# Last batch of an attention and feed-forward layer: tiles 4 and 5 turned by VectorE and moved inside SBUF in place of TensorE transposes, with other orders around them

## The chip, the cores and the metric

The kernel runs on one core of one Trainium2 chip. The metric is the device time of one execution, in microseconds (us); the figure quoted is the median of three runs. Five queues of instructions run side by side: TensorE (PE in the profile, its weight loads PEld), VectorE (DVE), ScalarE (ACT), GpSimd (POOL) and SyncE (SP), which issues nearly all DMAs. Each works through its own queue in order, and they wait for one another through semaphores.

## The reference

For 8 batches of 1024 rows of width 512, all in float32:

```
x  = x + layernorm(attn(layernorm(x)))
x  = x + layernorm(ffn(layernorm(x)))

attn(x): s  = sigmoid(silu(x @ s_w1.T + s_b1) @ s_w2.T + s_b2)
         u  = (x @ B_w.T + B_b) * s
         h  = h @ A.T + u_t            (a scan over the rows; 128 states)
         y  = hs @ C_w.T + C_b + x @ D_w.T + D_b
         return y * sigmoid(x @ g_w.T + g_b)
ffn(x):  square(relu(x @ Ws1)) @ Ws2   + a routed part weighted by trunc(prob)
```

The routed part counts only for rows whose largest probability reaches 1. A bound on the router's weights (`router_gap`, `route_flag`) tells at the end of the run whether any row can; if none can, that part is skipped, as in the runs shown.

## The kernel before

**Tiles.** A batch is 8 tiles (0 to 7) of 128 rows by 512. Batches run one after another; the last one has order lists of its own, `last_tail` and `last_body`, one in each engine's block, written out by hand call by call. What an engine does next is therefore fixed by these lists, and a call waits for its inputs with everything that stands behind it on that engine.

**One tile's way through the last batch.** TensorE computes the gate `G(j)` and the attention output `Y(j)`. ScalarE takes the sigmoid (`gate`). VectorE multiplies (`attn`, L1315), takes mean and variance (`v_bn`, `v_ag`, `v_ep`), subtracts the mean (`less_v_mean`), and adds the scaled result to x (`x1_sum`, L1346). GpSimd raises the variance to the power -1/2 in between (`v_rs`, L1942). Then VectorE takes the statistics of the sum (`x1_bn`, `x1_ag`, `x1_ep`), GpSimd makes scale and shift (`x1_rs`), and ScalarE writes the normed tile to `work` (`x1_norm`, L935).

**Turning a tile.** The feed-forward matmuls need the tile transposed, in a high part `x2T_hi` and a low part `x2T_lo` (float32 as two reduced parts, so each product is three matmuls, `mm3`, L499 to L501). Tiles 0 to 3 of the last batch, and all tiles of earlier batches, go this way: VectorE transposes 32x32 blocks into `x2q` (`turn`, L1369); when both tiles of a pair are there, SyncE issues four DMAs that carry the blocks to their partitions, back into `work` (`move`, L425); ScalarE copies the high part (`t_hi`, L926); GpSimd subtracts for the low part (`t_low`, L1997). Tiles 4 to 7 of the last batch go another way: `x1_norm` writes them with their columns permuted, TensorE transposes into PSUM banks (`T`, L579), ScalarE copies the high part from there (`t_hi`, L923), and VectorE subtracts (`t_low`, L1362).

**The feed-forward part.** `W1f(m, f)` (12 matmuls) multiplies half f of the hidden width for the four tiles of group m; its f = 0 call waits for the low part of the group's last tile. ScalarE applies relu and square (`hidden`, L968 and L971), VectorE squares in full precision and subtracts for the low part (`h2`, L1418 and L1422). `W2(j)` (6 matmuls) gives the output of tile j; `W2(0)` waits for `h2(0, 1)`. The output is normed (`z_bn`, `z_ag`, `z_ep` on VectorE, `z_rs` on GpSimd, `zn` on ScalarE), added to x (`outs` on GpSimd, `last_outs` and `very_last_out` on VectorE), and stored by SyncE.

**The order around the change.** On TensorE the last batch ends Y(4) to Y(7), W1f(0,0), W1f(0,1), T(4), T(5), W2(0), T(6), W2(1), T(7), W2(2), W1f(1,0), W1f(1,1), the router's matmuls, W2(3) to W2(7). On GpSimd it has `v_rs(5)`, `t_low(2)`, `t_low(3)`, `v_rs(6)`. On VectorE `h2(0,0)` stands behind `v_ep(7)` and ahead of `x1_sum(7)`, and `h2(0,1)` behind `x1_bn(7)`. `move` is called for tiles 0 to 3 only.

Of the kernel before, what the change touches and what calls it, by code (L numbers as in the profile page):

```python
# [18 lines left out]
def build(nc, x, xt, A, AT, BwT, Bb, CwT, Cb, DwT, Db, s1T, s1b, s2T, s2b, gwT, gb, Ws1p, Ws1, Ws2, W1, W2, Wr, eye, out):  # L19
    NB, T, D = x.shape  # L20
# [18 lines left out]
    with ExitStack() as ctx:  # L39
# [241 lines left out]

        def tr_bank(name):
            return TR[int(name[1]) % len(TR)]
# [77 lines left out]
        def _(eng):  # L361
# [65 lines left out]
            def one_pass(b, rep):  # L427
                if rep == 0:

                    eng.wait_ge(*lo_of("g"))  # L430
                    eng.wait_ge(*lo_of("d"))
                for m in range(NM):
                    js = slice(m * MS, (m + 1) * MS)
                    if rep > 0:
                        if m == NM - 1:
                            store_out(b - 1, 2)
                            store_out(b - 1, 3)
                        eng.wait_ge(S["x1_st" + str(m)], body_at("x1_st" + str(m), b - 1))
                        eng.wait_ge(S["out_ok"], body_at("out_ok", b - 1, m * MS + MS - 1))
                    eng.dma_start(xres[:, js, :], x_v[b][:, js, :]).then_inc(S[f"xres_ld{m}"], 16)  # L440
                    if rep + 1 < NB:
                        norm_rows(b, m)
                for m in range(NM):
                    js = slice(m * MS, (m + 1) * MS)
                    if rep + 1 < NB or m == 0:
                        move(b, 2 * m)
                    if rep + 2 < NB:
                        load_next_x(b + 2, m)
                    if rep + 1 < NB or m == 0:
                        move(b, 2 * m + 1)  # L450
                    eng.wait_ge(S["x1_ok"], body_at("x1_ok", b, m * MS + MS - 1))
                    eng.dma_start(x1_v[b][:, js, :], xres[:, js, :]).then_inc(S[f"x1_st{m}"], 16)
                store_out(b, 0)
                store_out(b, 1)
# [40 lines left out]
        def _(eng):  # L495
# [86 lines left out]
            def T(b, rep, j):  # L582

                if j >= MS + len(TR):
                    eng.wait_ge(S["t_lo"], body_at("t_lo", b, j - len(TR)))
                eng.wait_ge(S["xn2_ok"], body_at("xn2_ok", b, j))
                transposes(tr_bank(f"t{j}"), work[:, j, :]).then_inc(S["t_done"], 1)
# [181 lines left out]
            def last_body(b, rep):  # L769
                a = (b, rep)  # L770
                Y(*a, 0)
                G(*a, 4)
                Y(*a, 1)
                G(*a, 5)
                Y(*a, 2)
                Y(*a, 3)
                G(*a, 6)
                G(*a, 7)
                Y(*a, 4)
                Y(*a, 5)  # L780
                Y(*a, 6)
                Y(*a, 7)
                W1f(*a, 0, 0)
                W1f(*a, 0, 1)
                T(*a, 4)
                T(*a, 5)
                W2(*a, 0)
                T(*a, 6)
                W2(*a, 1)
                T(*a, 7)  # L790
# [88 lines left out]
        def _(eng):  # L879
# [32 lines left out]
            def t_hi(b, rep, j):  # L912
                if rep == NB - 1 and j >= MS:
                    eng.wait_ge(S["t_done"], j - MS + 1)
                else:
                    wait_moved(eng, b, j)
# [5 lines left out]
                if rep == NB - 1 and j >= MS:  # L922
# [5 lines left out]
            def x1_norm(b, rep, j):  # L928
                eng.wait_ge(S["x1_nm"], body_at("x1_nm", b, j))
                dst, src = work[:, j, :], xres[:, j, :]  # L930
                if rep == NB - 1 and j >= MS:

                    dst = dst.rearrange("p (k r q) -> p k q r", k=KD, q=4)
                    src = src.rearrange("p (k q r) -> p k q r", k=KD, q=4)
# [156 lines left out]
            def last_body(b, rep):  # L1091
                a = (b, rep)
                gate(*a, 4)
                hs(*a, 2)
                gate(*a, 5)
                hs(*a, 3)
                hs(*a, 4)
                x1_norm(*a, 0)
# [5 lines left out]
                x1_norm(*a, 3)  # L1104
                hs(*a, 6)
                t_hi(*a, 1)
                gate(*a, 7)
                hs(*a, 7)
                t_hi(*a, 2)
                t_hi(*a, 3)  # L1110
                x1_norm(*a, 4)
                hidden(*a, 0, 0)
                x1_norm(*a, 5)
                hidden(*a, 0, 1)
                t_hi(*a, 4)
                x1_norm(*a, 6)
                t_hi(*a, 5)
                x1_norm(*a, 7)
# [87 lines left out]
        def _(eng):  # L1206
# [507 lines left out]
            def last_body(b, rep):  # L1714
                a = (b, rep)
                attn(*a, 0)
                attn(*a, 1)
                v_bn(*a, 0)
                hs_low(*a, 2)
                v_bn(*a, 1)  # L1720
                v_ag(*a, 0)
                v_ep(*a, 0)
                less_v_mean(*a, 0)
                v_ag(*a, 1)
                v_ep(*a, 1)
                x1_sum(*a, 0)
                less_v_mean(*a, 1)
                hs_low(*a, 3)
                x1_sum(*a, 1)
                x1_bn(*a, 0)  # L1730
                x1_bn(*a, 1)
                x1_ag(*a, 0)
                x1_ep(*a, 0)
                attn(*a, 2)
                x1_ag(*a, 1)
                x1_ep(*a, 1)
                v_bn(*a, 2)
                hs_low(*a, 4)
                v_ag(*a, 2)
                v_ep(*a, 2)  # L1740
                attn(*a, 3)
                less_v_mean(*a, 2)
                x1_sum(*a, 2)
                turn(*a, 0)
                turn(*a, 1)
                v_bn(*a, 3)
                hs_low(*a, 5)
                v_ag(*a, 3)
                v_ep(*a, 3)
                less_v_mean(*a, 3)  # L1750
                x1_bn(*a, 2)
                x1_ag(*a, 2)
                x1_ep(*a, 2)
                x1_sum(*a, 3)
                x1_bn(*a, 3)
                x1_ag(*a, 3)
                x1_ep(*a, 3)
                turn(*a, 2)
                attn(*a, 4)
                turn(*a, 3)  # L1760
                hs_low(*a, 6)
                v_bn(*a, 4)
# [4 lines left out]
                x1_sum(*a, 4)  # L1767
                v_bn(*a, 5)
                v_ag(*a, 5)
                hs_low(*a, 7)  # L1770
# [5 lines left out]
                v_bn(*a, 6)  # L1776
                x1_ag(*a, 4)
                v_ag(*a, 6)
                x1_bn(*a, 5)
                x1_ep(*a, 4)  # L1780
                v_ep(*a, 6)
                less_v_mean(*a, 6)
                x1_ag(*a, 5)
                attn(*a, 7)
                v_bn(*a, 7)
                x1_sum(*a, 6)
                x1_ep(*a, 5)
                v_ag(*a, 7)
                x1_bn(*a, 6)
                less_v_mean(*a, 7)  # L1790
                x1_ag(*a, 6)
                v_ep(*a, 7)
                h2(*a, 0, 0)
                x1_sum(*a, 7)
                x1_ep(*a, 6)
                x1_bn(*a, 7)
                h2(*a, 0, 1)
                x1_ag(*a, 7)
                x1_ep(*a, 7)
                t_low(*a, 4)  # L1800
                t_low(*a, 5)
                z_bn(*a, 0)
                z_ag(*a, 0)
                z_ep(*a, 0)
                t_low(*a, 6)
                z_bn(*a, 1)
                t_low(*a, 7)
# [64 lines left out]
            h2(NB, NB, 1, 0)  # L1872
            z_ag(NB - 1, NB - 1, 2)
            z_ep(NB - 1, NB - 1, 2)
            h2(NB, NB, 1, 1)
            z_bn(NB - 1, NB - 1, 3)
            z_ag(NB - 1, NB - 1, 3)
# [7 lines left out]
            route_flag()  # L1885
# [49 lines left out]
        def _(eng):  # L1935
# [142 lines left out]
            def last_body(b):  # L2078
                v_rs(b, 0)
                v_rs(b, 1)  # L2080
                x1_rs(b, 0)
                v_rs(b, 2)
# [8 lines left out]
                t_low(b, 2)  # L2091
                t_low(b, 3)
                v_rs(b, 6)
# [4 lines left out]
                x1_rs(b, 7)  # L2098
                z_rs(b, 0)
# [69 lines left out]
```

## Time and profile before

| what | value |
|---|---|
| median of 3 runs | 800.47 us (800.14 to 800.48) |
| the profiled execution, its own time | 800.6 us |
| its span, first to last instruction | 798.6 us |
| TensorE busy | 783.3 us (98% of the span) |
| VectorE, GpSimd, ScalarE busy | 605.9, 456.4, 344.4 us |
| mean granted TensorE clock | 0.998 |

The profile is one execution, so times on its axis are compared with its own 800.6 us; it lies 0.13 us above the median. The last batch begins near 699 us, and the lists that the change touches work from about 729 us to the end. In a timeline each row is one instruction, or several alike that were merged (x2, x8); rows of VectorE and ScalarE that follow without a wait overlap a little, so that the step from one start to the next is shorter than the duration.

### The profile page before, as it was taken

To read this page: it belongs to the slowest core of one execution; us is meant where nothing else is said; L and a number is where in the kernel's file an instruction comes from. 1 tells how busy PE (TensorE), PEld (TensorE's weight loads), DVE (VectorE), ACT (ScalarE), POOL (GpSimd) and SP (SyncE) were. 2 spreads that over 40 slices of the span, in tenths; PEclk is the share of its full clock that TensorE was granted. 3 is DMA by queue.
4 is the path that set the end of the run, shared out by engine and by line. 5 is a ranking of instruction groups with operands and counts; after the bars stand their busy time and mean duration, and the time that the engine had idled before them with its cause. 6 is when DMAs were issued, how large, how long until landed. Compare 5 with 4: busy or idle time off the path is not lost. (4 is left out here: it accounts for less than half of the span.)

```text
span 798.6 us, 10778 instructions
## 1 busy us (share of the span) xinstructions
PE 783.3 (98%) x3628; PEld 648.0 (81%) x3628; DVE 605.9 (76%) x1404; ACT 344.4 (43%) x554; POOL 456.4 (57%) x553
## 2 busy tenths in 40 slices
PE   7999999999999999999999999999999999999996
PEld 6878888888888888888888888888888888888875
DVE  7868896598956897678975889649896589734895
ACT  4535354344434554245443535435443444432353
POOL 1253658548465576466674665845757557644445
PEclk9999999999999999999999999999999999999999
DMA  8534434454355425552345533454425442232222
GB/s 269 207 107 158 137 94 138 160 184 134 87 177 174 161 89 158 183 187 80 95 143 185 185 101 96 147 185 168 149 80 182 150 143 80 78 133 87 65 113 106
DMA packets 40767, 110.90 MB, mean 139 GB/s; under 512 B 7044, under 2 KB 24836, under 8 KB 32903
## 3 DMA queue, kind: packets, MB, share of 16 engines
q1 hardware_dynamic: 40278, 110.00, 41.4%
q8 instruction: 29, 0.48, 0.3%
q10 hardware_dynamic: 432, 0.20, 0.1%
q14 instruction: 28, 0.22, 0.1%
HBM read 60.84 MB, written 33.61 MB: 118 GB/s over the span
## 5 line engine op out<-in xcount | busy, mean ns | idle before, releaser
L499 PE MATMUL TM<-gw_hi,xT_hi 128*128 128x512 f32 x256 | 107.3, 419 | 0.0
L1982 POOL TENSOR_TENSOR xres<-work,xres 128x512 f32<-128x512 f32 x56 | 75.1, 1341 | 52.8 <-DVE work L1332 52.8
L501 PE MATMUL TM<-gw_hi,xT_lo 128*128 128x512 f32 x256 | 100.6, 393 | 0.0
L501 PE MATMUL TM<-dw_hi,xT_lo 128*128 128x512 f32 x256 | 100.2, 391 | 0.0
L500 PE MATMUL TM<-gw_lo,xT_hi 128*128 128x512 f32 x256 | 100.0, 391 | 0.0
L499 PE MATMUL TM<-dw_hi,xT_hi 128*128 128x512 f32 x256 | 99.9, 390 | 0.0
L500 PE MATMUL TM<-dw_lo,xT_hi 128*128 128x512 f32 x256 | 99.6, 389 | 0.0
L996 ACT ACTIVATE work<-TM,nmz,rsz 128x512 f32<-128x512 f32 x62 | 48.2, 777 | 106.7 <-POOL nmz L1952 106.7
L1942 POOL TENSOR_TENSOR rsv<-rsv,negh 128x1 f32<-128x1 f32 x64 | 47.1, 736 | 82.3 <-DVE rsv L1328 82.2
L1997 POOL TENSOR_TENSOR x2T_lo<-work,x2T_hi 128x512 fp32r<-128x512 f32 x60 | 78.5, 1319 | 2.0 <-ACT x2T_hi L926 1.9
L1990 POOL TENSOR_TENSOR work<-work,xres 128x512 f32<-128x512 f32 x60 | 76.7, 1295 | 1.3 <-ACT work L996 1.3
L1315 DVE TENSOR_TENSOR work<-TM,work 128x512 f32<-128x512 f32 x64 | 44.0, 687 | 43.9 <-PE TM L501 43.9
L1942 POOL TENSOR_TENSOR rsz<-rsz,negh 128x1 f32<-128x1 f32 x64 | 35.5, 555 | 59.1 <-DVE rsz L1470 58.5
L935 ACT ACTIVATE work<-xres,nmx,rsx 128x512 f32<-128x512 f32 x64 | 54.0, 843 | 32.8 <-POOL nmx L1952 32.7
L1254 DVE TENSOR_TENSOR xin<-xin,norm_row 128x1024 f32<-128x1024 f32 x56 | 66.1, 1211 | 0.4 <-ACT norm_row L941 0.3
L1942 POOL TENSOR_TENSOR rsx<-rsx,negh 128x1 f32<-128x1 f32 x64 | 40.6, 635 | 39.7 <-DVE rsx L1359 39.7
L926 ACT ACTIVATE x2T_hi<-work 128x512 fp32r<-128x512 f32 x60 | 36.1, 625 | 57.1 <-DMA work<-x2q 57.1
L501 PEld LDWEIGHTS TM<-gw_hi,xT_lo 128*128 128x128 f32 x256 | 48.0, 188 | 10.9
L501 PEld LDWEIGHTS TM<-dw_hi,xT_lo 128*128 128x128 f32 x256 | 48.1, 188 | 10.1
L500 PEld LDWEIGHTS TM<-dw_lo,xT_hi 128*128 128x128 f32 x256 | 48.1, 188 | 10.0
L499 PEld LDWEIGHTS TM<-dw_hi,xT_hi 128*128 128x128 f32 x256 | 48.1, 188 | 10.0
L901 ACT ACTIVATE work<-TM 128x512 f32<-128x512 f32 x64 | 37.2, 591 | 41.6 <-PE TM L501 36.3
(189 smaller groups left out, 2063.1 us busy)
## 6 DMA issues: line engine op xcount, KB each, us to landing
xres<-in_x SPq DMA_DIRECT2D x16, 1024.0 KB, 5.9
x_scratch<-xres SPq DMA_DIRECT2D x16, 1024.0 KB, 4.7
xin<-in_x SPq DMA_DIRECT2D x15, 1024.0 KB, 5.3
work<-x2q SPq DMA_DIRECT2D x120, 128.0 KB, 2.7
out<-work SPq DMA_DIRECT2D x30, 512.0 KB, 3.2
xin<-in_x_t SPq DMA_DIRECT2D x14, 1024.0 KB, 6.2
rows_in<-ln_scratch SPq DMA_DIRECT2D x14, 512.0 KB, 4.7
xin<-in_x SPq DMA_DIRECT2D x2, 512.0 KB, 5.0
```

Of the source, the lines that this page charges most:

```text
L499: eng.matmul(ps, lhs[0], rhs[0], start=first, stop=False)
L500: eng.matmul(ps, lhs[0], rhs[1], start=False, stop=False)
L501: return eng.matmul(ps, lhs[1], rhs[0], start=False, stop=last)
L901: eng.activation(work[:, j, :], tm_bank(f"g{j}")[:, :], ACT.Sigmoid).then_inc(S["gate_ok"], 1)
L935: eng.activation(dst, src, ACT.Identity, bias=nmx[:, j:j + 1], scale=rsx[:, j:j + 1])\
L996: eng.activation(work[:, j, :], z_bank(rep, j)[:, :], ACT.Identity, bias=nmz[:, j:j + 1], scale=rsz[:, j:j + 1]).then_inc(S["zn_ok"], 1)
L1254: return eng.tensor_tensor(xT, xT, r.unsqueeze(2).to_broadcast([P, 2, KD, P]), op)
L1315: eng.tensor_tensor(work[:, j, :], tm_bank(f"y{j}")[:, :], work[:, j, :], ALU.mult)\
L1942: return eng.tensor_tensor(dst, src, negh[:, 0:n], ALU.pow)
L1982: eng.tensor_tensor(xres[:, j, :], work[:, j, :], xres[:, j, :], ALU.add).then_inc(S["x1_ok"], 1)
L1990: eng.tensor_tensor(work[:, j, :], work[:, j, :], xres[:, j, :], ALU.add).then_inc(S["out_ok"], 1)
L1997: eng.tensor_tensor(by_blocks(x2T_lo[:, j % MS, :, :]), moved_tile(j), by_blocks(x2T_hi[:, j % MS, :, :]).bitcast(F32), ALU.subtract).then ...
```

## The change

Tiles 4 and 5 of the last batch take the way of tiles 0 to 3: block transposes on VectorE, four more DMAs inside SBUF, high parts from `work`, low parts on GpSimd. Only tiles 6 and 7 are still transposed by TensorE, ahead of W2(0) and W2(1). The order lists of all engines in the last batch are changed as well: on GpSimd `v_rs(2)` and `v_rs(6)` each move up one place; on VectorE the two new `turn` calls and the rest of tile 7's statistics come ahead of `h2(0,0)`; `route_flag` moves up from behind `z_ep(5)` to behind `z_bn(3)`.

```diff
@@ -279,6 +279,8 @@
             return PREP_BANKS[name] if rep < 0 and name in PREP_BANKS else FM[slot(FM_RING, name)]
+        TURNED = 6
+
         def tr_bank(name):
             return TR[int(name[1]) % len(TR)]
@@ -442,8 +444,7 @@
                         norm_rows(b, m)
                 for m in range(NM):
                     js = slice(m * MS, (m + 1) * MS)
-                    if rep + 1 < NB or m == 0:
-                        move(b, 2 * m)
+                    move(b, 2 * m)
                     if rep + 2 < NB:
                         load_next_x(b + 2, m)
                     if rep + 1 < NB or m == 0:
@@ -581,7 +582,7 @@
             def T(b, rep, j):
-                if j >= MS + len(TR):
+                if j >= TURNED + len(TR):
                     eng.wait_ge(S["t_lo"], body_at("t_lo", b, j - len(TR)))
                 eng.wait_ge(S["xn2_ok"], body_at("xn2_ok", b, j))
                 transposes(tr_bank(f"t{j}"), work[:, j, :]).then_inc(S["t_done"], 1)
@@ -782,12 +783,10 @@
                 Y(*a, 7)
                 W1f(*a, 0, 0)
                 W1f(*a, 0, 1)
-                T(*a, 4)
-                T(*a, 5)
+                T(*a, 6)
                 W2(*a, 0)
-                T(*a, 6)
+                T(*a, 7)
                 W2(*a, 1)
-                T(*a, 7)
             assert len(POWERS) == 21
             busy(9)
@@ -910,8 +909,8 @@
                 eng.activation(hs_hi[:, j % 2, :], src, ACT.Copy).then_inc(S["hs_hi_ok"], 1)
             def t_hi(b, rep, j):
-                if rep == NB - 1 and j >= MS:
-                    eng.wait_ge(S["t_done"], j - MS + 1)
+                if rep == NB - 1 and j >= TURNED:
+                    eng.wait_ge(S["t_done"], j - TURNED + 1)
                 else:
                     wait_moved(eng, b, j)
@@ -919,7 +918,7 @@
                     eng.wait_ge(S["w1_done"], body_at("w1_done", b - 1, KF * NM - 1))
                 elif j % MS == 0 and j:
                     eng.wait_ge(S["w1_done"], body_at("w1_done", b, KF * (j // MS) - 1))
-                if rep == NB - 1 and j >= MS:
+                if rep == NB - 1 and j >= TURNED:
                     eng.activation(x2T_hi[:, j % MS, :, :], tr_bank(f"t{j}")[:, :].rearrange("p (k n) -> p k n", n=P),
                                    ACT.Copy).then_inc(S["t_hi"], 1)
                 else:
@@ -928,7 +927,7 @@
             def x1_norm(b, rep, j):
                 eng.wait_ge(S["x1_nm"], body_at("x1_nm", b, j))
                 dst, src = work[:, j, :], xres[:, j, :]
-                if rep == NB - 1 and j >= MS:
+                if rep == NB - 1 and j >= TURNED:
                     dst = dst.rearrange("p (k r q) -> p k q r", k=KD, q=4)
                     src = src.rearrange("p (k q r) -> p k q r", k=KD, q=4)
@@ -1090,32 +1089,32 @@
             def last_body(b, rep):
                 a = (b, rep)
+                hs(*a, 2)
                 gate(*a, 4)
-                hs(*a, 2)
+                hs(*a, 3)
                 gate(*a, 5)
-                hs(*a, 3)
+                x1_norm(*a, 0)
                 hs(*a, 4)
-                x1_norm(*a, 0)
                 x1_norm(*a, 1)
                 gate(*a, 6)
                 hs(*a, 5)
                 x1_norm(*a, 2)
                 t_hi(*a, 0)
                 x1_norm(*a, 3)
+                gate(*a, 7)
                 hs(*a, 6)
+                hs(*a, 7)
                 t_hi(*a, 1)
-                gate(*a, 7)
-                hs(*a, 7)
                 t_hi(*a, 2)
                 t_hi(*a, 3)
                 x1_norm(*a, 4)
+                x1_norm(*a, 5)
                 hidden(*a, 0, 0)
-                x1_norm(*a, 5)
+                x1_norm(*a, 6)
                 hidden(*a, 0, 1)
+                x1_norm(*a, 7)
                 t_hi(*a, 4)
-                x1_norm(*a, 6)
                 t_hi(*a, 5)
-                x1_norm(*a, 7)
                 t_hi(*a, 6)
                 t_hi(*a, 7)
                 zn(*a, 0)
@@ -1714,97 +1713,97 @@
...
                 turn(*a, 2)
                 attn(*a, 4)
                 turn(*a, 3)
+                v_bn(*a, 4)
                 hs_low(*a, 6)
-                v_bn(*a, 4)
                 v_ag(*a, 4)
                 v_ep(*a, 4)
                 less_v_mean(*a, 4)
                 attn(*a, 5)
-                x1_sum(*a, 4)
+                hs_low(*a, 7)
                 v_bn(*a, 5)
                 v_ag(*a, 5)
-                hs_low(*a, 7)
+                x1_sum(*a, 4)
                 less_v_mean(*a, 5)
                 v_ep(*a, 5)
                 x1_bn(*a, 4)
                 attn(*a, 6)
                 x1_sum(*a, 5)
                 v_bn(*a, 6)
+                v_ag(*a, 6)
                 x1_ag(*a, 4)
-                v_ag(*a, 6)
+                v_ep(*a, 6)
                 x1_bn(*a, 5)
+                less_v_mean(*a, 6)
                 x1_ep(*a, 4)
-                v_ep(*a, 6)
-                less_v_mean(*a, 6)
+                attn(*a, 7)
+                x1_sum(*a, 6)
+                v_bn(*a, 7)
                 x1_ag(*a, 5)
-                attn(*a, 7)
-                v_bn(*a, 7)
-                x1_sum(*a, 6)
+                v_ag(*a, 7)
                 x1_ep(*a, 5)
-                v_ag(*a, 7)
                 x1_bn(*a, 6)
+                v_ep(*a, 7)
                 less_v_mean(*a, 7)
                 x1_ag(*a, 6)
-                v_ep(*a, 7)
+                turn(*a, 4)
+                x1_ep(*a, 6)
+                x1_sum(*a, 7)
+                turn(*a, 5)
+                x1_bn(*a, 7)
+                x1_ag(*a, 7)
                 h2(*a, 0, 0)
-                x1_sum(*a, 7)
-                x1_ep(*a, 6)
-                x1_bn(*a, 7)
+                x1_ep(*a, 7)
                 h2(*a, 0, 1)
-                x1_ag(*a, 7)
-                x1_ep(*a, 7)
-                t_low(*a, 4)
-                t_low(*a, 5)
                 z_bn(*a, 0)
+                t_low(*a, 6)
+                t_low(*a, 7)
                 z_ag(*a, 0)
                 z_ep(*a, 0)
-                t_low(*a, 6)
                 z_bn(*a, 1)
-                t_low(*a, 7)
                 z_ag(*a, 1)
                 z_ep(*a, 1)
@@ -1869,11 +1868,12 @@
             last_tail(NB - 1, NB - 1)
             last_body(NB - 1, NB - 1)
             z_bn(NB - 1, NB - 1, 2)
-            h2(NB, NB, 1, 0)
             z_ag(NB - 1, NB - 1, 2)
             z_ep(NB - 1, NB - 1, 2)
+            h2(NB, NB, 1, 0)
             h2(NB, NB, 1, 1)
             z_bn(NB - 1, NB - 1, 3)
+            route_flag()
             z_ag(NB - 1, NB - 1, 3)
             z_ep(NB - 1, NB - 1, 3)
             z_bn(NB, NB, 4)
@@ -1882,7 +1882,6 @@
             z_bn(NB, NB, 5)
             z_ag(NB, NB, 5)
             z_ep(NB, NB, 5)
-            route_flag()
             z_bn(NB, NB, 6)
             z_ag(NB, NB, 6)
             z_ep(NB, NB, 6)
@@ -2078,8 +2077,8 @@
             def last_body(b):
                 v_rs(b, 0)
                 v_rs(b, 1)
+                v_rs(b, 2)
                 x1_rs(b, 0)
-                v_rs(b, 2)
                 x1_rs(b, 1)
                 v_rs(b, 3)
                 x1_rs(b, 2)
@@ -2089,13 +2088,15 @@
                 t_low(b, 1)
                 v_rs(b, 5)
                 t_low(b, 2)
+                v_rs(b, 6)
                 t_low(b, 3)
-                v_rs(b, 6)
                 x1_rs(b, 4)
                 x1_rs(b, 5)
                 v_rs(b, 7)
                 x1_rs(b, 6)
                 x1_rs(b, 7)
+                t_low(b, 4)
+                t_low(b, 5)
                 z_rs(b, 0)
                 z_rs(b, 1)
                 outs(b, 0)
```

## Rows read from the trace of the kernel before

**Rows 1.** Waits of TensorE, 735 to 799 us: us in total, times, longest.
```profile
PE TM L499 <- DVE h_lo L1422: 1.5, 1, 1.5
```

**Rows 2.** Timeline of TensorE: start us, us, instruction, [idle before <- releaser].
```profile
764.16 0.50 PE L499 MATMUL FM<-x2T_hi,f1w_hi 128*128 128x512 f32 x1
...
769.74 1.03 PE L579 MATMUL TR<-ident,work 128*128 128x128 f32 x8
772.23 0.50 PE L499 MATMUL TM<-f2w_hi,h_hi 128*128 128x512 f32 x1 [1.46 <-DVE h_lo L1422]
...
773.73 0.60 PE L579 MATMUL TR<-ident,work 128*128 128x128 f32 x4
774.08 0.48 PE L499 MATMUL TM<-f2w_hi,h_hi 128*128 128x512 f32 x1
...
777.15 0.40 PE L501 MATMUL TM<-f2w_hi,h_lo 128*128 128x512 f32 x1
777.57 0.50 PE L499 MATMUL FM<-x2T_hi,f1w_hi 128*128 128x512 f32 x1
```

**Rows 3.** Timeline of GpSimd, 761 to 766 us.
```profile
761.11 3.00 POOL L1997 TENSOR_TENSOR x2T_lo<-work,x2T_hi 128x512 fp32r<-128x512 f32 x2
764.54 0.72 POOL L1942 TENSOR_TENSOR rsv<-rsv,negh 128x1 f32<-128x1 f32 x1 [0.43 <-DVE rsv L1328]
```

**Rows 4.** Timeline of VectorE, 761 to 772 us.
```profile
761.03 0.67 DVE L1315 TENSOR_TENSOR work<-TM,work 128x512 f32<-128x512 f32 x1
761.62 1.33 DVE L1346 SCALAR_TENSOR_TENSOR xres<-work,rsv,xres 128x512 f32<-128x512 f32 x1
762.87 0.68 DVE L1320 BATCH_NORM_STATS2 st<-work 128x6 f32<-128x512 f32 x1
...
763.59 0.18 DVE L1324 BATCH_NORM_AGGREGATE mvv<-st 128x2 f32<-128x6 f32 x1
...
766.16 0.73 DVE L1346 SCALAR_TENSOR_TENSOR xres<-work,rsv,xres 128x512 f32<-128x512 f32 x1
...
768.06 0.68 DVE L1418 SCALAR_TENSOR_TENSOR w_first<-FM,hf 128x512 f32<-128x512 f32 x1
...
770.78 0.67 DVE L1418 SCALAR_TENSOR_TENSOR w_first<-FM,hf 128x512 f32<-128x512 f32 x1
771.49 0.69 DVE L1422 TENSOR_TENSOR h_lo<-w_first,h_hi 128x512 fp32r<-128x512 f32 x1
```

**Rows 5.** Timeline of ScalarE, 769 to 771 us.
```profile
769.93 0.60 ACT L968 ACTIVATE hf<-FM 128x512 f32<-128x512 f32 x1
```

**Rows 6.** Timeline of all engines, 754 to 761 us.
```profile
754.57 0.70 DVE L1369 STREAM_TRANSPOSE x2q<-work 128x512 f32<-128x512 f32 x1
...
760.07 1.15 ACT L926 ACTIVATE x2T_hi<-work 128x512 fp32r<-128x512 f32 x2 [2.36 <-DMA work<-x2q]
```

**Rows 7.** Instructions of the tile x2q, whole span: ns min/median/max; who waited (us, times); landing us.
```profile
L425 SPq DMA_DIRECT2D work<-x2q x120: 543/605/1567, 80.2 to 757.2; - x120
...
  ACT x2T_hi L926: 57.1, 23
...
DMA to landing us min/median/max: 2.5/2.7/3.6
```

**Rows 8.** Timeline of VectorE, 787 to 790 us.
```profile
787.14 0.70 DVE L1462 BATCH_NORM_STATS2 st<-TM 128x6 f32<-128x512 f32 x1 [0.42 <-PE TM L501]
...
788.51 0.70 DVE L1462 BATCH_NORM_STATS2 st<-TM 128x6 f32<-128x512 f32 x1 [0.26 <-PE TM L501]
...
789.53 0.22 DVE L1437 TENSOR_REDUCE gap_max<-SC 128x1 f32<-128x64 f32 x1
...
789.96 0.69 DVE L1462 BATCH_NORM_STATS2 st<-TR 128x6 f32<-128x512 f32 x1
```

**Rows 9.** Windows: stretch, us, busy by engine (x), granted clock, DMA share, GB/s.
```profile
770.00:773.00 3.00, 1.54 (x11) 1.21 (x9) 2.93 (x8) 2.97 (x5) 1.27 (x3) 1.00 0.72 298
...
792.00:799.00 7.00, 0.00 (x0) 0.00 (x0) 3.12 (x7) 1.37 (x2) 1.09 (x3) 0.77 0.53 195
```

More of the change, by code:

```diff
@@ L1716, in last_body @@
                 attn(*a, 0)
+                v_bn(*a, 0)
+                v_ag(*a, 0)
                 attn(*a, 1)
-                v_bn(*a, 0)
                 hs_low(*a, 2)
                 v_bn(*a, 1)
-                v_ag(*a, 0)
                 v_ep(*a, 0)
+                v_ag(*a, 1)
                 less_v_mean(*a, 0)
-                v_ag(*a, 1)
                 v_ep(*a, 1)
                 x1_sum(*a, 0)
+                x1_bn(*a, 0)
+                x1_ag(*a, 0)
                 less_v_mean(*a, 1)
@@ L1729, in last_body @@
                 x1_sum(*a, 1)
-                x1_bn(*a, 0)
+                x1_ep(*a, 0)
                 x1_bn(*a, 1)
-                x1_ag(*a, 0)
-                x1_ep(*a, 0)
                 attn(*a, 2)
+                v_bn(*a, 2)
+                v_ag(*a, 2)
+                less_v_mean(*a, 2)
+                v_ep(*a, 2)
                 x1_ag(*a, 1)
                 x1_ep(*a, 1)
-                v_bn(*a, 2)
+                attn(*a, 3)
+                x1_sum(*a, 2)
+                v_bn(*a, 3)
+                v_ag(*a, 3)
                 hs_low(*a, 4)
[L1739 to L1743, printed above, removed]
                 turn(*a, 0)
+                v_ep(*a, 3)
                 turn(*a, 1)
[L1746 to L1749, printed above, removed]
                 less_v_mean(*a, 3)
+                x1_sum(*a, 3)
                 x1_bn(*a, 2)
+                x1_bn(*a, 3)
                 x1_ag(*a, 2)
                 x1_ep(*a, 2)
-                x1_sum(*a, 3)
-                x1_bn(*a, 3)
                 x1_ag(*a, 3)
+                hs_low(*a, 5)
                 x1_ep(*a, 3)
```

## Prediction

> **What bounds the kernel now.** I read the page first, for the busy shares; then the waits of TensorE in the last batch; then the timelines of TensorE, VectorE, GpSimd and ScalarE over that stretch; then the tile that the new transfers use. TensorE is busy for 98% of the span, as the table above has it, and from 735 us on its matmul queue waits visibly only once, 1.5 us [rows 1]. That is the place of the change: after W1f(0,1) TensorE does T(4) and T(5), eight transposes from 769.74 us, then stands until W2(0) at 772.23, because `h2(0,1)` on VectorE ends at 772.18 [rows 2, 4]. VectorE is back to back there, so from about 761 to 772 us the order of its list decides; everything behind W2(0) is TensorE's pace again. So the end moves by what W1f(1,0), at 777.57 us now [rows 2], moves, if nothing behind it changes. Between W2(0) and W1f(1,0), T(6) and T(7) cost TensorE time that no wait hides.
>
> **The change, part by part.**
>
> *GpSimd, `v_rs(6)` ahead of `t_low(3)`.* Now `t_low(2)` and `t_low(3)` run from 761.11 to 764.11, then `v_rs(6)` at 764.54 [rows 3], and W1f(0,0), which needs `t_low(3)`, starts at 764.16 [rows 2]. In the new order `v_rs(6)` comes first. It needs `v_ep(6)`, behind `v_bn(6)`, which runs on VectorE from 762.87 to 763.55 [rows 4], and behind three short instructions, each like the 0.18 us one at 763.59, of which one waits for the one before: ready near 763.95 [rows 4]. VectorE's queue up to `v_bn(6)` holds the same calls as before, in a slightly other order, so I leave that time. Start about 764.0, 0.55 us for the power (the 0.72 in that row was a disturbed one), `t_low(3)` from 764.55, and half of the 3.00 us less the shared part, 1.3 us: 765.85. W1f(0,0) starts near 765.9, which is 1.7 us later. Queued behind `t_low(3)` on GpSimd are the scale and shift of tiles 4 and 5, which ScalarE's `x1_norm` and then `turn` wait for; counted the same way they are ready some 0.4 us ahead of `turn(4)`'s place on VectorE, and would cost VectorE one for one if not.
> Its relu of the second half then starts at 765.9 + (769.93 - 764.16) = 771.7 [rows 2, 5], ends at 772.3, and the two VectorE instructions of `h2(0,1)` need 771.49 - 770.78 + 0.69 = 1.40 us more: 773.7. So the late start is swallowed only in part by the stall before W2(0).
>
> *VectorE, more ahead of `h2(0,0)`.* Now `h2(0,0)` starts at 768.06 [rows 4]. The new list has in addition, ahead of it, two `turn` calls, `x1_sum(7)`, `x1_bn(7)`, `x1_ag(7)` and `x1_ep(6)`. A full-width instruction of 0.70 us steps by about 0.61; `turn` is one of them, at 0.70 [rows 6], and `x1_sum` is at 0.73 [rows 4]. That makes 2 x 0.61 + 0.66 + 0.61 + 0.2 + 0.07 = 2.76 us. `x1_sum(6)` now overlaps the late `t_low(3)`; beside `t_low(2)` such a sum took 1.33 us and alone 0.73 [rows 4], and since only the last 0.3 us of `t_low(3)` overlap I take 0.1 for it. `h2(0,0)` then starts at 768.06 + 2.76 + 0.1 = 770.9. Two halves of 1.40 us, and 0.15 for `x1_ep(7)` between them and the hand-over to TensorE, give W2(0) at 773.85. This is later than the 773.7 of the other chain, so it decides: W2(0) is 1.6 us late, against 772.23.
> The Trainium skill (SBUF — State Buffer, "Who interferes with whom") says that a VectorE instruction with two SBUF inputs and a GpSimd one that reads SBUF exclude each other, and that the later one fully blocks. The row agrees in direction: `x1_sum(5)`, with both inputs in SBUF, is the slow one, and `attn(6)` beside the same GpSimd work, with one input in PSUM, took 0.67 us [rows 4]. By the full block the 0.1 us above would be 0.3 and the sum below 0.2 larger.
>
> *TensorE, T(4) and T(5) gone.* In the stall they cost nothing, so leaving them out saves nothing. But T(6) moves into their place, and from W2(0) to W1f(1,0) only T(7) is left. With two transposes the way was 772.23 to 777.38 (the last matmul at 777.15 plus one step of 0.23), 5.15 us [rows 2]. One transposed tile costs 774.08 - 773.73 = 0.35 us plus about 0.1 that the matmul behind it starts slower: 0.45. New way 4.70, so TensorE is at W1f(1,0) at 773.85 + 4.70 = 778.55.
>
> *The way through SBUF for tiles 4 and 5.* `turn(5)` steps out 0.8 us ahead of `h2(0,0)` (`x1_bn(7)` and `x1_ag(7)` between) and ends near 770.2. For the pair before, `turn` ended at 755.27 and `t_hi(2)` started at 760.07: 4.80 us [rows 6], of which four DMA issues at 0.605 us and 2.7 us to landing are the bulk [rows 7]. So `t_hi(4)` starts at 775.0, `t_hi(5)` 0.55 later, and GpSimd's low parts run from 775.7 to 778.3 at 1.3 each. `t_hi(6)`, `t_hi(7)` queue behind on ScalarE, and their low parts on VectorE end near 778.1. All of it is ahead of 778.55, by 0.25 us: hidden, thinly. SyncE's queue holds one 1 MB store behind these DMAs, and nobody waits for that store before the end.
> W1f(1,0) is thus 778.55 - 777.57 = 0.98 us late.
>
> *`route_flag` earlier.* At 789.53 it stands between `z_ep(5)` and `z_bn(6)`, and `z_bn(6)` starts at 789.96; at TensorE's pace of 788.51 - 787.14 = 1.37 us it could at 789.88 [rows 8]. Gain 0.08. In its new place it has the 0.42 us of idle ahead of `z_bn(4)` [rows 8] to lie in; it lasts 0.43, so at most 0.05 is lost there, in a stretch that waits for TensorE again 1.4 us later.
>
> *The other orders* (tiles 0 to 3, ScalarE's list) move waits inside a stretch where TensorE has no gap: from 735 to 764 us the waits name none [rows 1]. If that cover went, each late `hs_low` would cost one for one; by my count of the new lists the nearest has some 3 us to spare. ScalarE's `x1_norm` of tiles 4 and 5, now unpermuted, is shorter, and ScalarE has time there.
>
> **Sum.** +0.98 - 0.08 = +0.9. The profiled execution would go from 800.6 to 801.5 us, and the median, 0.13 lower, from 800.47 to 801.4.
>
> **Bounds.** Low: `x1_sum(5)` meets less of GpSimd's work and saves its 0.6 us; then both chains come 0.6 sooner, W2(0) at 773.2, and the sum is +0.3: 800.8. High: the landing is the slowest of the 120, 3.6 against 2.7 [rows 7], which puts the low part of tile 5 at 779.2, and `x1_sum(6)` takes 1.33 too, which adds 0.6 to both ways: W1f(1,0) at 779.8, sum +2.1: 802.6.
>
> **Rivals.**
> *The transposes' gain comes through.* If VectorE reaches `h2(0,1)` as early as now and the DMAs land early, only the 0.45 and the 0.08 remain, and the 0.19 us between 777.38 and 777.57 that W1f(1,0) waits now [rows 2] go as well: -0.7, 799.8 us. For it: TensorE is the busiest engine, and each transpose taken off it counts. Against it: 2.8 us more stand ahead of `h2(0,0)`. Decided if W2(0) starts before 772.9.
> *Slower by over 0.2%: the transfers set W1f(1,0).* From the point where the low part of tile 5 is later than 778.55, each further us is a us at the end; from 779.2 on the loss passes 1.6 us. For it: the cover is 0.25 us, and ScalarE waited 23 times, 57.1 us in all, for these DMAs in this trace [rows 7], so they are often last. Against it: the last pair took the ordinary time. With 1 us more W1f(1,0) is at 779.3, the sum +1.65, the time 802.1 us.
> *The clock falls.* Two stalls of TensorE of some 1.7 us each lie 6 us apart. Now the granted clock stays at 1.00 through the stall, with 1.54 us of work in 3, and is below 1 only in the stretch behind the last matmul (0.77 as a mean) [rows 9]. At the lower of the two levels, 1.2 instead of 2.4 GHz, W2(0)'s 1.37 us would double, and the sum be +2.3: 802.8 us. The Trainium skill (TensorE: Matmul & The Clock Gate, "What's actually happening") says that idleness throttles TensorE and activity releases it; this trace shows the fall only at its end.
>
> **Chances.** Forecast, +0.3 to +1.6: 0.72. Gain comes through: 0.08. Transfers late: 0.15. Clock: 0.03. Something else, either way: 0.02. About 0.2%, 1.6 us, is what a measurement of this kernel can tell from no change. The forecast lies inside it; of the late transfers most lie beyond, as does the clock. So: faster 0.03, same 0.80, slower 0.17. Range: 800.1, into the first rival, to 802.5, near the upper bound; the rest is under 2 in 10.
>
> **What would show it.** Right: W1f(0,0) with a gap of about 1.7 us before it, released by GpSimd's `x2T_lo`; W2(0) 1.6 us later, released by VectorE's `h_lo`; one transposed tile between W2(0) and W2(1) and none behind; W1f(1,0) about 1 us later. Wrong: no gap before W1f(0,0) would refute the GpSimd step; W2(0) near 772 the VectorE count; W1f(1,0) released by `x2T_lo` of GpSimd long after TensorE is free would be the transfers. The prediction fails if VectorE's list up to `v_bn(6)`, which I left unmoved, runs otherwise than counted.

## The result: slower by 2.7 us, outside the range

| | before | after |
|---|---|---|
| median, beside one another on one chip | 800.42 us (6 runs, 800.14 to 800.51) | 803.1 us (6 runs, 802.7 to 804.48) |
| ratio after / before, 95% interval | | 1.0038 [1.0027, 1.0048] |
| the profiled execution, its own time | 800.6 us | 802.89 us |
| its span | 798.6 us | 801.1 us |
| mean granted TensorE clock | 0.998 | 0.995 |

The interval lies wholly above 1.002, so this is the "slower" case, which I had given 0.17, and 803.1 is above the range's upper end of 802.5. Lines of the kernel after are one lower than before on the helpers shown (L1421 is `h2`'s second instruction, L1996 GpSimd's `t_low`), one higher on TensorE (L500 to L502, L580).

I read the waits of TensorE first, from 735 to 799 us; the columns are those of [rows 1].

```profile
PE FM L500 <- POOL x2T_lo L1996: 2.0, 1, 2.0
PE TM L500 <- DVE h_lo L1421: 1.6, 1, 1.6
```

There are two waits where there was one: the new one is in front of W1f(0,0), and the old one in front of W2(0) is still there, slightly longer. The timeline of TensorE in the kernel after, against [rows 2]:

```profile
763.76 0.40 PE L502 MATMUL TM<-cw_hi,hs_lo 128*128 128x512 f32 x1
766.13 0.50 PE L500 MATMUL FM<-x2T_hi,f1w_hi 128*128 128x512 f32 x1 [1.97 <-POOL x2T_lo L1996]
766.47 0.55 PE L501 MATMUL FM<-x2T_lo,f1w_hi 128*128 128x512 f32 x1
766.82 0.63 PE L502 MATMUL FM<-x2T_hi,f1w_lo 128*128 128x512 f32 x1
767.24 0.63 PE L500 MATMUL FM<-x2T_hi,f1w_hi 128*128 128x512 f32 x1
...
769.80 0.47 PE L500 MATMUL FM<-x2T_hi,f1w_hi 128*128 128x512 f32 x1
770.11 0.39 PE L501 MATMUL FM<-x2T_lo,f1w_hi 128*128 128x512 f32 x1
...
773.29 0.66 PE L580 MATMUL TR<-ident,work 128*128 128x128 f32 x4
775.59 0.50 PE L500 MATMUL TM<-f2w_hi,h_hi 128*128 128x512 f32 x1 [1.65 <-DVE h_lo L1421]
...
780.29 0.39 PE L500 MATMUL FM<-x2T_hi,f1w_hi 128*128 128x512 f32 x1
```

The first row is the last matmul of Y(7). W1f(0,0) starts 1.97 us later than before (766.13 against 764.16). But between 766.82 and 769.80 seven matmuls step by 0.43 us each instead of 0.23, with durations of 0.63 instead of 0.39. That is the lower clock level, as the windows of the same stretch show (columns as in [rows 9]; the column behind the engines is the granted clock):

```profile
764.00:766.00 2.00, 0.16 (x1) 0.00 (x0) 2.00 (x5) 0.00 (x0) 1.95 (x2) 1.00 0.00 0
766.00:767.00 1.00, 0.87 (x3) 0.73 (x4) 1.00 (x2) 0.00 (x0) 1.00 (x2) 0.77 0.00 0
767.00:768.00 1.00, 1.00 (x4) 0.81 (x3) 1.00 (x5) 0.46 (x1) 0.72 (x3) 0.50 0.00 0
...
769.00:770.00 1.00, 1.00 (x4) 0.81 (x3) 0.98 (x4) 0.53 (x1) 0.84 (x2) 0.52 0.00 0
770.00:772.00 2.00, 2.00 (x11) 1.65 (x10) 1.97 (x5) 1.21 (x3) 0.71 (x2) 1.00 0.03 5
...
774.00:776.00 2.00, 0.41 (x2) 0.37 (x3) 1.38 (x2) 1.97 (x4) 0.00 (x0) 1.00 1.01 362
```

The same matmuls in the kernel before, its timeline of TensorE and then its windows:

```profile
766.79 0.39 PE L501 MATMUL FM<-x2T_hi,f1w_lo 128*128 128x512 f32 x1
767.01 0.39 PE L499 MATMUL FM<-x2T_hi,f1w_hi 128*128 128x512 f32 x1
```

```profile
764.00:770.00 6.00, 6.00 (x29) 4.83 (x28) 5.93 (x17) 3.65 (x5) 3.04 (x7) 1.00 0.00 0
```

0.50 is 1.2 GHz in place of 2.4. The engine stood for 1.97 us, worked for about 0.4 us at full clock, and then ran at the lower level until just before 770 us, although it was busy all that time. The second stall, 1.65 us in front of W2(0), left the clock at 1.00.

Now the path to W2(0), on ScalarE and VectorE of the kernel after (both engines in one view), against [rows 4, 5]:

```profile
771.39 0.69 DVE L1417 SCALAR_TENSOR_TENSOR w_first<-FM,hf 128x512 f32<-128x512 f32 x1
...
773.48 0.60 ACT L967 ACTIVATE hf<-FM 128x512 f32<-128x512 f32 x1 [0.24 <-PE FM L502]
774.11 0.69 DVE L1417 SCALAR_TENSOR_TENSOR w_first<-FM,hf 128x512 f32<-128x512 f32 x1 [1.23 <-ACT hf L967]
774.84 0.69 DVE L1421 TENSOR_TENSOR h_lo<-w_first,h_hi 128x512 fp32r<-128x512 f32 x1
```

`h2(0,1)` waits 1.23 us for the relu, and the relu waits for TensorE. So it is not VectorE's list that set W2(0), as I had forecast, but TensorE's own late and slow W1f, through the relu. The relu is 3.55 us later than before (773.48 - 769.93): 1.97 of it is the start of W1f(0,0), the other 1.58 the lower clock. W2(0) is then 3.36 us late (775.59 - 772.23). From W2(0) to W1f(1,0) it takes 4.70 us (780.29 - 775.59) where it took 5.34, so W1f(1,0) is 2.72 us late. The end follows, a little less late: the span grew by 2.5 us.

### The profile page after: what moved, and what is told of

Its sections match the earlier page's. It is cut to its first block, busy times and chain, and to the rows that moved or that the text cites. A ratio compares the mean times of both kernels' runs of the same rounds, so it can differ in the third digit from the quotient of the medians.

```text
span 801.1 us, 10767 instructions
## 1 busy us (share of the span) xinstructions
PE 783.3 (98%) x3620; PEld 647.5 (81%) x3620; DVE 606.5 (76%) x1404; ACT 343.8 (43%) x554; POOL 459.8 (57%) x555
## 4 chain that ended last, share of the span: by engine, by line
PE 95%; DVE 2%; ACT 1%; DMA 1%; issue 0%; POOL 0%; DVEq 0%
PE TM L500 20%; PE TM L502 20%; PE TM L501 20%; PE FM L500 9%; PE FM L502 9%; PE FM L501 9%; PE SC L544 2%; PE SC L536 2%; PE SC L540 1%; PE FM L689 1%; PE FM L686 1%; PE FM L687 1%; DMA xin<-in_x 1%; PE TM L580 0%; DVE st L1219 0%
## 5 line engine op out<-in xcount | busy, mean ns | idle before, releaser
L500 PE MATMUL TM<-gw_hi,xT_hi 128*128 128x512 f32 x256 | 107.3, 419 | 0.0
L502 PE MATMUL TM<-gw_hi,xT_lo 128*128 128x512 f32 x256 | 100.7, 393 | 0.0
L502 PE MATMUL TM<-dw_hi,xT_lo 128*128 128x512 f32 x256 | 100.2, 391 | 0.0
L500 PE MATMUL TM<-dw_hi,xT_hi 128*128 128x512 f32 x256 | 99.9, 390 | 0.0
L1996 POOL TENSOR_TENSOR x2T_lo<-work,x2T_hi 128x512 fp32r<-128x512 f32 x62 | 81.0, 1316 | 6.0 <-ACT x2T_hi L925 6.0
L502 PEld LDWEIGHTS TM<-gw_hi,xT_lo 128*128 128x128 f32 x256 | 48.0, 188 | 10.9
L502 PEld LDWEIGHTS TM<-dw_hi,xT_lo 128*128 128x128 f32 x256 | 48.1, 188 | 10.2
L500 PEld LDWEIGHTS TM<-dw_hi,xT_hi 128*128 128x128 f32 x256 | 48.1, 188 | 9.9
```

The lines of the kernel that those rows point to most:

```text
L500: eng.matmul(ps, lhs[0], rhs[0], start=first, stop=False)
L502: return eng.matmul(ps, lhs[1], rhs[0], start=False, stop=last)
L1996: eng.tensor_tensor(by_blocks(x2T_lo[:, j % MS, :, :]), moved_tile(j), by_blocks(x2T_hi[:, j % MS, :, :]).bitcast(F32), ALU.subtract).then ...
```

## The experiments

Each kernel ran beside the kernel before on the same chip; the ratio is to that, with its 95% interval, and the clock behind a time is the mean of that run. The first four ran together, then three, then two. The `fill` matmuls write into a PSUM bank that is free then, and nothing reads them.

**1. The GpSimd order put back in the kernel after.**

```diff
                 t_low(b, 2)
-                v_rs(b, 6)
                 t_low(b, 3)
+                v_rs(b, 6)
```

> The changed kernel with one pair on GpSimd put back: t_low(3) ahead of v_rs(6). Theory A (this pair makes a stall of about 2 us ahead of W1f(0,0), after which the granted clock falls for some 3.4 us and costs 1.6 us more): W1f(0,0) starts by 764.5, the clock is 1.00 from 764 to 770, W2(0) starts near 774.2, set by VectorE's longer list, and the time is near 801.3 us. If the stall that then lies ahead of W2(0) lets the clock fall there instead, near 802.6. Theory B (the two turns on VectorE and the transfers account for the loss, the pair on GpSimd for next to nothing): 802.7 or more, as for the changed kernel, with W2(0) still near 775.6.

Measured: 802.75 us (7 runs, 801.35 to 803.74), ratio 1.0031 [1.002, 1.0043]. One run took 801.35 us at clock 0.998; the other six lie at 802.67 to 803.74 with 0.994 to 0.997. The profile is of the 801.35 run; its timeline of TensorE:

```profile
764.05 0.50 PE L500 MATMUL FM<-x2T_hi,f1w_hi 128*128 128x512 f32 x1
...
771.84 0.66 PE L580 MATMUL TR<-ident,work 128*128 128x128 f32 x4 [2.05 <-ACT work L934]
773.95 0.50 PE L500 MATMUL TM<-f2w_hi,h_hi 128*128 128x512 f32 x1 [1.45 <-DVE h_lo L1421]
...
778.68 0.39 PE L500 MATMUL FM<-x2T_hi,f1w_hi 128*128 128x512 f32 x1
```

The wait ahead of W1f(0,0) is gone, as it should be, but the idle time only moves: TensorE is at T(6) early and stands 2.05 us there, then 1.45 us more. Where the clock held, as in this run, VectorE's list alone gives W2(0) at 773.95 and W1f(1,0) at 778.68, 1.11 us late; the forecast had 773.85 and 778.55. That the six other runs lost their 1.3 to 2.4 us to the clock rests on their mean clock; where in the span it fell in them no trace shows (experiment 5 comes back to this).

**2. The GpSimd order alone, in the kernel before.**

```diff
                 t_low(b, 2)
-                t_low(b, 3)
                 v_rs(b, 6)
+                t_low(b, 3)
```

> The kernel before with that one pair on GpSimd in the new order: v_rs(6) ahead of t_low(3), nothing else. Theory A: a stall of 2 us ahead of W1f(0,0), then the granted clock at 0.5 for about 3.4 us, W2(0) near 775.6, W1f(1,0) near 780.7, and 803.4 us. A without the fall of the clock: W2(0) near 774.0, and 801.9 us. Theory B: within 0.5 us of the kernel before, 800.4 to 800.9 us.

Measured: 803.79 us (5 runs, 802.33 to 804.3), ratio 1.0033 [1.0019, 1.0048], all five at clock 0.995 to 0.997. One pair of lines exchanged costs the kernel before about as much as the whole change: its median is 3.4 us above that of the kernel before beside it (800.37), with five runs that spread over 2 us. Its timeline and then its windows:

```profile
766.85 0.51 PE L499 MATMUL FM<-x2T_hi,f1w_hi 128*128 128x512 f32 x1 [2.30 <-POOL x2T_lo L1997]
```

```profile
766.00:768.00 2.00, 1.15 (x5) 0.97 (x6) 2.00 (x5) 0.00 (x0) 1.79 (x3) 1.00 0.00 0
768.00:770.00 2.00, 2.00 (x7) 1.56 (x6) 0.59 (x4) 1.30 (x1) 1.79 (x4) 0.56 0.00 0
770.00:772.00 2.00, 2.00 (x6) 1.53 (x6) 0.11 (x1) 0.71 (x2) 0.00 (x0) 0.59 0.00 0
772.00:774.00 2.00, 2.00 (x10) 1.64 (x9) 1.96 (x4) 1.74 (x2) 0.00 (x0) 1.00 0.00 0
```

The same stall, and behind it the same fall: the first five matmuls still run at 1.00, and then, from about 768.2 to 771.6 us, come some 3.4 us at the lower level.

**3. and 4. The kernel after, with unused matmuls in the stalls.** Experiment 3 has only the first call of `fill`, experiment 4 both.

```diff
+            def fill(n):
+                for _ in range(n):
+                    eng.matmul(TR[1][:, :], xT_hi[:, L - 1, 0, :], d_w[0][:, 0:D], start=True, stop=True)
...
                 Y(*a, 7)
+                fill(8)
                 W1f(*a, 0, 0)
                 W1f(*a, 0, 1)
                 T(*a, 6)
+                fill(7)
                 W2(*a, 0)
```

> The changed kernel with eight matmuls of 128x512 on data that nobody uses, written to a PSUM bank that is free then, put ahead of W1f(0,0): they fill most of the stall of 2.0 us and end before t_low(3) does, so no wait is shortened. Theory A: W1f(0,0) still starts near 766.1, the granted clock stays at 1.00, W1f(0,1) ends 1.6 us earlier, W2(0) starts near 774.3, set by VectorE, and the time is near 801.7 us. Theory B: the clock has no share in it, and the time stays at 803 us.

> As the kernel with the first stall filled, and seven more such matmuls between T(6) and W2(0). If the second stall, about 2 us once the first is filled, lets the clock fall at W2(0), this one is faster than that with the first stall filled by about 1.4 us, at 801.7 us; if the second stall costs no clock, the two are equal within 0.3 us.

Measured, experiment 3: 801.89 us (10 runs), ratio 1.0026 [1.0016, 1.0036]. Six runs are at 801.58 to 801.94 with clock 0.998 or more, four at 803.19 to 804.9 with 0.994 to 0.996. Its profile is of one of the four (803.74); the timeline of TensorE and the windows:

```profile
766.49 0.50 PE L500 MATMUL FM<-x2T_hi,f1w_hi 128*128 128x512 f32 x1 [0.17 <-POOL x2T_lo L2002]
...
772.68 0.66 PE L580 MATMUL TR<-ident,work 128*128 128x128 f32 x4 [0.46 <-ACT work L940]
774.78 0.77 PE L500 MATMUL TM<-f2w_hi,h_hi 128*128 128x512 f32 x1 [1.45 <-DVE h_lo L1427]
```

```profile
766.00:770.00 4.00, 3.83 (x17) 2.92 (x16) 3.98 (x12) 1.74 (x3) 3.35 (x7) 1.00 0.00 0
...
776.00:778.00 2.00, 2.00 (x7) 1.52 (x7) 0.27 (x1) 1.63 (x4) 1.28 (x2) 0.50 0.73 303
```

With the first stall filled W1f(0,0) is no earlier (766.49), but it runs at 1.00; in this run the clock fell behind the second stall instead, at W2(0), which is where my clock rival had put it.

Measured, experiment 4: 801.73 us (10 runs, 801.29 to 802.14), ratio 1.0016 [1.0006, 1.0025], every run at clock 0.997 to 0.999. In its timeline of TensorE:

```profile
766.47 0.50 PE L500 MATMUL FM<-x2T_hi,f1w_hi 128*128 128x512 f32 x1 [0.17 <-POOL x2T_lo L2003]
...
774.77 0.49 PE L500 MATMUL TM<-f2w_hi,h_hi 128*128 128x512 f32 x1
...
779.48 0.39 PE L500 MATMUL FM<-x2T_hi,f1w_hi 128*128 128x512 f32 x1
```

The matmuls of `fill` compute nothing that is used, and W1f(0,0) starts no earlier with them (766.47), so only the clock can have gained from them: 803.1 - 801.73 = 1.4 us of the change's 2.7 us, and most of the scatter. The traces give a little less. From W1f(0,0) to W2(0) it takes 8.30 us here (774.77 - 766.47) and 9.46 in the kernel after (775.59 - 766.13), so 1.16 of the 1.58 us of clock reached the end; the rest is covered, because with the clock held `h_lo` on VectorE, which ends at 774.70 here, sets W2(0) again. What is left, 801.73 - 800.37 (the kernel before, run beside it) = 1.4 us, is the late work itself.

**5. Experiment 1 with its stalls filled** (`fill(8)` ahead of `T(6)`, `fill(6)` behind it, GpSimd's order as in the kernel before).

> The changed kernel with t_low(3) ahead of v_rs(6) again on GpSimd, and unused matmuls of 128x512 in the stall that is then left: eight between W1f(0,1) and T(6), six between T(6) and W2(0), all ending before what follows is ready. Theory A (the forecast's sum of waits holds as long as the clock holds): clock 1.00 throughout, W2(0) near 774.0 set by VectorE, W1f(1,0) near 778.7, and 801.2 us in nearly every run, against 802.7 with the same order unfilled. Theory B (the runs at 802.7 have another cause than the clock): the same spread as unfilled, 801.3 to 803.7.

Measured: 801.43 us (10 runs, nine of them 801.15 to 801.7), ratio 1.0013 [1.0004, 1.0023]. Put beside experiment 4, the GpSimd exchange with a held clock is worth 0.3 us, and beside experiment 1 the filling gains 1.3 us. Nine of ten runs near 801.4, against six of seven above 802.6 in experiment 1, also tie the loss there to the stalls: the fall at the start that the last section describes is out of the filling's reach, and here it shows in the one run at 802.7. This kernel's time is the forecast's 801.4, but the forecast was made for the kernel with the GpSimd exchange.

**6. One instruction more on VectorE, on top of experiment 5.**

```diff
                 turn(*a, 5)
+                eng.bn_stats(st6[:, 0, 0, :], xres[:, 0, :])
                 x1_bn(*a, 7)
```

> As the filled kernel with the order put back, with one more VectorE instruction (statistics of a tile that nobody uses, 0.61 us a step) between turn(5) and x1_bn(7), so ahead of h2(0,0) and not ahead of the transfers. If VectorE's list ahead of h2(0,0) sets W2(0), as the forecast counted, the time is 0.6 us longer than the filled kernel's: 801.8. If the transfers of tiles 4 and 5 set the end, it is the same within 0.2 us: 801.2.

Measured: 802.18 us (10 runs), ratio 1.0025 [1.0016, 1.0035], 0.75 us above experiment 5. In its timeline W2(0) still waits for VectorE's `h_lo`:

```profile
775.08 0.50 PE L500 MATMUL TM<-f2w_hi,h_hi 128*128 128x512 f32 x1 [1.01 <-DVE h_lo L1428]
```

So with the clock held an instruction ahead of `h2(0,0)`, which steps by some 0.6 us, reaches the end at its full price, and the two `turn` calls of the change stand in the same place. The trace has in addition a wait of 0.45 us ahead of `h2(0,1)`, which experiment 1's has not; why, no run shows.

**7. The new transfers later, on top of experiment 5** (the last batch's second `move` behind the store of x1 on SyncE, not ahead of it).

> As the filled kernel with the order put back, with the four DMAs of tiles 4 and 5 behind the 1 MB store of x1 on SyncE's queue instead of ahead of it. The store delays them by its issue, 0.6 us, and by what the two share of the DMA engines, so the low part of tile 5 comes 0.6 to 3 us later, against a cover of some 0.2 us. If the cover is as thin as the forecast counted, W1f(1,0) waits for GpSimd's low part and the time is 0.4 to 2.8 us longer than the filled kernel's: 801.6 to 804.0. If the transfers have room, it is the same within 0.2 us.

Measured: 802.53 us (8 runs), ratio 1.0026 [1.0016, 1.0037], 1.1 us above experiment 5. Its timeline:

```profile
781.55 0.50 PE L503 MATMUL FM<-x2T_hi,f1w_hi 128*128 128x512 f32 x1 [1.01 <-POOL x2T_lo L2006]
```

Here the rival of the late transfers comes true: W1f(1,0) waits for GpSimd's low part. (This run also had the start-up fall described at the end, which shifts the axis: W1f(0,0) starts at 765.76, 1.7 us later than in experiment 1.) As the change places them the transfers are hidden, but only just.

**8. The kernel before with its one stall filled** (`fill(5)` between `T(5)` and `W2(0)`). Some runs of the kernel before too lie near 801.5 to 802.0 at clock 0.996.

> The kernel before with five unused matmuls of 128x512 between T(5) and W2(0), in its stall of 1.46 us. 4 of 23 runs of the kernel before took 801.5 us or more at a lower mean clock (0.996). If that is the clock falling in this stall too, the filled kernel has no such run and the same median, 800.3 to 800.5 us. If not, it has them as often.

Measured: 800.41 us (11 runs), ratio 0.9997 [0.9988, 1.0006]. The one run at 801.62 remained, and it is the one profiled. Its windows at the start and in the last batch:

```profile
18.00:21.00 3.00, 3.00 (x10) 2.52 (x11) 2.85 (x7) 0.00 (x0) 0.23 (x1) 0.53 1.02 391
21.00:24.00 3.00, 3.00 (x18) 2.56 (x17) 2.44 (x2) 0.93 (x2) 0.00 (x0) 0.90 1.08 376
...
764.00:772.00 8.00, 8.00 (x40) 6.43 (x40) 7.92 (x23) 4.72 (x6) 4.54 (x9) 1.00 0.02 10
```

Of the two outcomes expected the second came: the median is that of the kernel before beside it (800.44), and one longer run in 11 is about as often as three in 21 there (801.76 to 801.99). So no cost of this stall through the clock is seen, and the rare longer runs, as far as this one trace shows, have their fall at the start.

**9. A try for a faster kernel: experiment 8 with `h2(0,1)` one call earlier and the change's `route_flag` place.**

```diff
                 x1_ep(*a, 6)
-                x1_bn(*a, 7)
                 h2(*a, 0, 1)
+                x1_bn(*a, 7)
...
             z_bn(NB - 1, NB - 1, 3)
+            route_flag()
...
-            route_flag()
             z_bn(NB, NB, 6)
```

> As the kernel before with its stall filled, with h2(0,1) ahead of x1_bn(7) on VectorE and route_flag behind z_bn(3). By the same count W2(0) comes 0.2 us earlier and the end gains 0.08 us from the flag: 800.1 us. If x1_norm(7), which comes later by some 0.4 us, then holds up T(7), the gain is lost: 800.4.

Measured: 800.71 us (11 runs), ratio 1.0003 [0.9994, 1.0012]: no gain, and 0.3 us above the higher of the two times expected. In its timeline TensorE waits at W1f(1,0) instead:

```profile
778.18 0.50 PE L499 MATMUL FM<-x2T_hi,f1w_hi 128*128 128x512 f32 x1 [0.24 <-DVE x2T_lo L1369]
```

What was taken from W2(0)'s wait came back as a wait for the last tile's low part, whose statistics now come later. No version that beats the kernel before was found.

## Why the prediction was wrong

**The step that failed is the one that kept TensorE at full clock** in the sum, and gave the rival "the clock falls" 0.03. I had one row for it, the kernel before at 1.00 through a stall of 1.46 us with some work around it [rows 2, 9], and read from it that a stall of 1.7 us ahead of W1f(0,0) would pass as well. In the kernel after the stall was 1.97 us with no work in it at all, and the clock fell in the profiled run: the matmuls of W1f took 1.58 us longer, of which 1.2 (by the traces) to 1.4 us (by the medians) reached the end. All six runs have a mean clock of 0.994 to 0.996. Experiments 3 and 4 show the cause, since filling the stalls alone brings the time from 803.1 to 801.73 us; experiment 2 shows that the GpSimd exchange is enough to set it off. The rival itself came out at 802.8 against 803.1, but that is luck in part: it was put at W2(0), whose 1.37 us it doubled. In the kernel after the clock falls one stall earlier, where it also takes the place of VectorE as what sets W2(0).

**The other steps, one by one.**
- *GpSimd.* Right, a little small: `v_rs(6)` ran from 764.05 to 764.60 and `t_low(3)` to 766.08, forecast 765.85; its end fell beside `x1_sum(6)`, and it took 1.51 us where 1.3 were counted. Its timeline:

```profile
764.05 0.55 POOL L1941 TENSOR_TENSOR rsv<-rsv,negh 128x1 f32<-128x1 f32 x1 [1.64 <-DVE rsv L1327]
764.57 1.51 POOL L1996 TENSOR_TENSOR x2T_lo<-work,x2T_hi 128x512 fp32r<-128x512 f32 x1
```

- *VectorE's list.* Right in experiment 1 (`h2(0,0)` at 770.92, forecast 770.9, of which 0.1 was for an overlap that experiment 1 does not have). In the kernel after it is 0.5 us later, 771.39 in the row above. The term that was too small, for about half of that, is the overlap of `x1_sum(6)` with `t_low(3)`, which I had at 0.1 us. In VectorE's timeline of the kernel after it took 1.09 us, against 0.73 alone [rows 4]:

```profile
765.54 1.09 DVE L1345 SCALAR_TENSOR_TENSOR xres<-work,rsv,xres 128x512 f32<-128x512 f32 x1
```

  That is 0.36 more where I had 0.1. The two overlapped from 765.54 to 766.08, for 0.54 us and not for the 0.3 that I counted. By the Trainium skill's rule of the full block (SBUF — State Buffer, "Who interferes with whom") all of the overlap would be lost; the row agrees in direction, with 0.36 lost of 0.54, so that the 0.3 that the prediction had by this rule comes close by luck. With the other chain later still, it cost nothing in the kernel after.
- *One transposed tile less between W2(0) and W1f(1,0).* Right: 4.70 us in the kernel after, 4.73 in experiment 1, 4.71 in experiment 4, forecast 4.70.
- *Transfers.* Hidden as forecast, though 0.7 us later than counted. GpSimd's low parts of tiles 4 and 5, on its timeline of the kernel after, end at 778.99, forecast 778.3, and W1f(1,0) came 1.30 us behind them without waiting:

```profile
776.45 2.54 POOL L1996 TENSOR_TENSOR x2T_lo<-work,x2T_hi 128x512 fp32r<-128x512 f32 x2 [2.46 <-ACT x2T_hi L925]
```

  At full clock the cover is thin: in experiment 1 they end at 778.43 for W1f(1,0) at 778.68, which is the 0.25 us of the prediction, in experiment 4 at 779.27 for 779.48, and experiment 7 shows what happens without it.
- *`route_flag`.* Right: `z_bn(3)` is 2.59 us late, `z_bn(6)` 2.50, a gain of 0.09 against 0.08. `z_bn(6)`, which started behind the flag's work in [rows 8], now waits for TensorE. In VectorE's timeline of the kernel after:

```profile
788.21 0.70 DVE L1461 BATCH_NORM_STATS2 st<-TM 128x6 f32<-128x512 f32 x1 [0.22 <-PE TM L502]
788.83 0.21 DVE L1436 TENSOR_REDUCE gap_max<-SC 128x1 f32<-128x64 f32 x1
...
792.46 0.70 DVE L1461 BATCH_NORM_STATS2 st<-TR 128x6 f32<-128x512 f32 x1 [0.26 <-PE TR L502]
```

- *The sum.* At full clock it nearly holds. The kernel after itself with the clock held takes 801.73 us (experiment 4) against 801.4: the GpSimd exchange cost 0.3 us where the sum had 0.1 for it. Without the exchange it is 801.35 (experiment 1's one run) and 801.43 us (experiment 5). Experiment 5 differs from the kernel before by +1.1 us: the saved transposes do not pay for the two `turn` calls ahead of `h2(0,0)`. No run puts back the tiles or the other orders by themselves, so that these two make up the 1.1 us rests on the starts that the traces show and on experiment 6.

**What stays open.** Which stalls let the clock fall. 1.97 us (kernel after) and 2.30 (experiment 2) did in the traces; 1.46 (kernel before) and 1.65 (kernel after, at W2(0)) did not; 0.46 and 1.45 with one tile's transposes between did in experiment 3's trace, and not in all of its runs; 2.05 and 1.45 with the same between did not in experiment 1's trace, though most of its runs look as if they had. The length of the stall alone does not sort these. The Trainium skill (TensorE: Matmul & The Clock Gate, "What's actually happening") has idleness throttle and activity release; the rows agree in direction. They add that the fall came after work had resumed: about 0.4 us into it in the kernel after, more than 1 us into it in experiment 2, but less than 0.1 us into it at W2(0) in experiment 3. What the longest runs of the kernel after (803.79 and 804.48 us) lost beyond the profiled one, no trace shows.

## What to carry to other kernels

On an engine that is busy for 98% of the span, a new stall is to be priced twice: with its length, and with the matmuls behind it at half speed (here 1.97 us of wait and 1.58 us of clock; of the clock 1.2 to 1.4 us reached the end, since VectorE's longer list makes W2(0) late anyway); a trace in which one stall kept the clock is no cover for another. A call moved up one place ahead of a longer one on a helper engine has to be followed to the engine that waits for the longer one: exchanging `v_rs(6)` and `t_low(3)` alone cost the kernel before 3.4 us. Before judging a change by a fraction of a per cent, look at the mean clock of each run and fill the stalls once with unused matmuls: it separates the order's cost (1.4 us) from the clock's (1.4 us).

## What was not expected of the hardware

The clock also falls between 18 and 24 us, in start-up, in some runs, whether the last batch is that of the kernel before (experiment 8) or close to that of the kernel after (experiments 5 and 7). In experiment 8's trace it is 0.53 from 18 to 21 us, in experiment 5's 0.70 from 18 to 21 and 0.73 from 21 to 24, in experiment 7's 0.75 and 0.69; in the traces of the kernels before and after it is 1.00 there. In experiment 5's trace everything behind it is later by 1.4 us (W1f(0,0) at 765.42 against 764.05 in experiment 1), and that run took 802.7 us where its neighbours took 801.15 to 801.7. TensorE's work ahead of it is the same kind of short matmuls with a wait of 0.80 us in the traces with the fall and without.
